# GpSimd splits the maxima and divides the sums; the batch chain is laid over more steps; maxima run 30 ahead

## The reference

```
x = x + gelu(layernorm(x) @ ctx^T) @ ctx
x = x + router over 8 experts (gelu MLP, weighted) of layernorm(x)
q = layernorm(x) @ Wq^T ; k, v = ctx @ Wk^T, ctx @ Wv^T          (16 heads of 16)
x = x + softmax(where(mask, q k^T + bias[bucket(distance)], -1e9)) v @ Wo^T
h = layernorm(x); e = argmax of a small router on h's last row of each batch
x = x + h + 0.3 * ((gelu(h @ W1[e] + b1[e]) @ W2[e] + b2[e]) @ Wo + bo)
```

## Time and profile before

| | |
|---|---|
| median of 3 runs | 736.22 us (727.66 to 737.24) |
| profiled execution | 738.62 us, span of the core 736.8 us |
| PE, DVE, ACT, POOL busy | 650.3, 357.2, 262.1, 96.6 us |
| attention loop (64 steps) | about 416 to 653 us |

### The profile page before, as it was taken

How to read it: one execution, slowest core, us unless ns; L and a number is a source line. 1 busy time by engine, 2 the same in 40 slices (tenths; PEclk the granted TensorE clock), 3 DMA queues, 4 the chain that set the end, 5 groups by cost and what they waited for, 6 DMA issues and landing times.

```text
span 736.8 us, 8966 instructions
## 1 busy us (share of the span) xinstructions
PE 650.3 (88%) x3020; PEld 383.9 (52%) x3021; DVE 357.2 (48%) x1115; ACT 262.1 (36%) x353; POOL 96.6 (13%) x102
## 2 busy tenths in 40 slices
PE   3999999999997768999697898989887988799996
PEld 2666666666665447899673333333342333243644
DVE  4324423003036872232274878868878788423302
ACT  1111111111122322344215666636643675562220
POOL 0000000000020003545401503001006000303000
PEclk9999999999998998999988999979986999899999
DMA  9993105103001135222239524153161000302031
GB/s 313 362 348 124 65 1 180 64 0 118 0 1 62 56 121 118 74 64 77 68 117 127 84 34 78 39 85 68 17 126 23 2 1 2 115 2 57 1 114 57
DMA packets 48131, 61.96 MB, mean 84 GB/s; under 512 B 7959, under 2 KB 41272, under 8 KB 47688
## 3 DMA queue, kind: packets, MB, share of 16 engines
q1 hardware_dynamic: 45944, 55.66, 28.7%
q0 software_dynamic: 2144, 5.77, 2.7%
HBM read 43.89 MB, written 10.93 MB: 74 GB/s over the span
## 4 chain that ended last, share of the span: by engine, by line
PE 72%; DVE 16%; issue 4%; DMA 3%; ACT 3%; POOL 1%; DVEq 0%; POOLq 0%; ACTq 0%; SPq 0%
PE ps L859 13%; PE ps L870 12%; PE ps L1416 8%; PE ps L1398 6%; PE ps L1301 5%; PE ps L1133 4%; PE ps L1021 4%; DVE arena L2098 4%; PE ps L1029 3%; PE ps L1124 3%; DVE arena L1801 2%; PE ps L943 2%; PE ps L1143 2%; PE ps L1324 1%; PE ps L1049 1%
## 5 line engine op out<-in xcount | busy, mean ns | idle before, releaser
L1626 ACT ACTIVATE arena<-ps 100x1024 f32<-100x1024 f32 x128 | 124.6, 1021 | 81.8 <-PE ps L1398 81.6
L2098 DVE TENSOR_REDUCE arena<-ps 128x1 f32<-128x400 f32 x256 | 131.4, 566 | 32.2 <-PE ps L1301 30.2
L859 PE MATMUL ps<-xnT,arena 128*128 128x512 f32 x208 | 102.0, 616 | 0.9 <-DVE xnT L1686 0.9
L870 PE MATMUL ps<-arena 128*128 128x256 f32 x416 | 99.7, 384 | 0.0
L870 PEld LDWEIGHTS ps<-arena 128*128 128x128 f32 x416 | 80.6, 194 | 33.6 <-issue 25.0
L1454 ACT ACTIVATE arena<-ps 128x512 f32<-128x512 f32 x52 | 31.1, 597 | 175.8 <-PE ps L859 175.8
L1301 PE MATMUL ps<-arena 97*128 97x400 bf16 x256 | 79.4, 354 | 11.3 <-DVE arena L2098 8.2
L1398 PE MATMUL ps<-arena 100*100 100x512 bf16 x256 | 81.3, 403 | 0.7 <-DMA arena<-arena 0.5
L1416 PE MATMUL ps<-arena 100*32 100x512 f32 x512 | 76.3, 659 | 0.5 <-ACT arena L1626 0.5
L1301 PEld LDWEIGHTS ps<-arena 97*128 97x128 bf16 x256 | 20.9, 99 | 89.5 <-DVE arena L2098 56.8
L1686 DVE COPY xnT<-ps 128x512 f32<-128x512 f32 x16 | 10.4, 687 | 100.3 <-PE ps L832 100.3
(11 more groups left out here) (228 smaller groups left out, 701.9 us busy)
## 6 DMA issues: line engine op xcount, KB each, us to landing
arena<-in_W SPq DMA_DIRECT2D x16, 512.0 KB, 8.8
arena<-in_ctxT SPq DMA_DIRECT2D x4, 1664.0 KB, 8.5
arena<-in_ctxN SPq DMA_DIRECT2D x4, 1664.0 KB, 12.8
arena<-arena SPq DMA_DIRECT2D x48, 128.0 KB
arena<-in_pW SPq DMA_DIRECT2D x8, 512.0 KB, 4.3
last_k_parts<-arena SPq DMA_DIRECT2D x24, 100.0 KB, 1.8
arena<-last_k_parts SPq DMA_DIRECT2D x8, 300.0 KB
x_tok<-in_x SPq DMA_DIRECT2D x4, 512.0 KB, 9.3
```

The costliest lines, as they stand in the source:

```text
L859: ins = pe.matmul(ps[:, 4 + k % 2, :], ctxT_s[:, b % 2, c, f * P:f * P + P], xnT[:, c, S * b:S * b + S], start=(c == 0), stop=(c == KC - 1))
L870: ins = pe.matmul(ps[:, b % 2 * 2 + t // 2, t % 2 * D:t % 2 * D + D], hid[:, (k - 2) % 4, t * P:t * P + P], ctxN_s[:, b % 2, f, :], start= ...
L1626: act.activation(pexp2[0:KT, c % 4, :, :], ps[0:KT, 2 + 2 * (c % 2):4 + 2 * (c % 2), :], ACT.Exp).then_inc(f_pe, 1)
L2098: dve.tensor_reduce(nm2[:, h, j:j + 1], ps[:, FAST.bank(x), 0:KF], AX.X, ALU.max, negate=True).then_inc(s_by["dve"], 1)
```

## The change

Three things, in the fast way alone. LEAD goes from 28 to 30. GpSimd gets an order of its own by steps: it splits the maxima of the units from 2 on (the units 0 and 1 stay with VectorE), multiplies by the reciprocals that VectorE still takes (divide; turn_back waits for it), and does the last queries' split, the normalised rows and the final sums (in two halves) at given steps. The chain goes over more steps: projections at 3 and 5, roots at 6, 7, 9, 11, normalised rows at 12, turns at 13 and 14, sums at 13 and 15. nm2, rl2 are doubled. The router's loads stand behind maxima row 4 instead of 10.

```diff
-LEAD = 28
+LEAD = 30
+OWN_SPLITS = 2
...
-CHAIN = {3: ("project", 0), 4: ("project", 1), 10: ("turn4", 0), 12: ("turn4", 1)}
-ROOTS_AT = 4
+CHAIN = {3: ("project", 0), 5: ("project", 1), 13: ("turn4", 0), 14: ("turn4", 1)}
+ROOTS_AT = (6, 7, 9, 11)
+NORM_AT, BASE_AT = 12, (13, 15)
...
@@ SyncE, fast_way @@
-                    if w == 10:
+                    if w == 4:
                         router_weights()
...
@@ VectorE, maxima(m) @@
+                    if n == 0 and m >= 2 * MU:
+                        dve.wait_ge(s_nm, m // MU - 1)
+                    dve.tensor_reduce(nm2[:, m // MU % 2, h, j:j + 1], ps[:, FAST.bank(x), 0:KF], AX.X, ALU.max, negate=True).then_inc(s_by["dve"], 1)
...
-                def normalise(i):
-
-                    lo = i % 2 * DK
+                def invert_sums(i):
+
                     dve.wait_ge(f_oc, i + 1)
-                    cf.step(dve, dve.reciprocal(rl2[:, :, :], vt2[:, i % 2, :, DK:DK + 1]))
-                    cf.step(dve, dve.tensor_tensor(vn2[:, i // 2 % 2, :, lo:lo + DK], vt2[:, i % 2, :, 0:DK],
-                                                   rl2.broadcast_to([P, S // VW, DK]), ALU.mult))
+                    cf.add(dve.reciprocal(rl2[:, i % 2, :, :], vt2[:, i % 2, :, DK:DK + 1]))
+                    inverted[i] = cf.n

                 def turn_back(i):
...
+                    dve.wait_ge(f_div, i + 1)
...
-                    if t == 0 and u + 1 < UNITS:
+                    if t == 0 and 1 <= u + 1 < OWN_SPLITS:
                         split_maxima(u + 1)
...
@@ GpSimd @@
+            def fast_way():
+                steps = Chain(s_split)
+
+                def split_maxima(w):
+
+                    pool.wait_ge(s_by["dve"], FAST.taken(("max", MU * w + MU - 1))[1])
+                    pool.wait_ge(s_made, FAST.made(("max rows", w - 1)))
+                    nv, rv = nm2[:, w % 2, :, :].rearrange("p h j -> p j h"), nr2.rearrange("p h j -> p j h")
+                    steps.step(pool, pool.tensor_copy(nmb2[:, :, 0, :], nv))
+                    steps.step(pool, pool.tensor_tensor(rv, nv, nmb2[:, :, 0, :], ALU.subtract))
+                    steps.step(pool, pool.tensor_copy(nmb2[:, :, 1, :], rv))
+                    pool.tensor_tensor(nmb2[:, :, 2, :], rv, nmb2[:, :, 1, :], ALU.subtract).then_inc(s_nm, 1)
+
+                def divide(i):
+
+                    lo = i % 2 * DK
+                    pool.wait_ge(f_dv, inverted[i])
+                    pool.tensor_tensor(vn2[:, i // 2 % 2, :, lo:lo + DK], vt2[:, i % 2, :, 0:DK],
+                                       rl2[:, i % 2, :, :].broadcast_to([P, S // VW, DK]), ALU.mult).then_inc(f_div, 1)
+
+                late = [x for st in range(STEPS) for x in extras(st) if x[0] == "products"]
+                for use in range(KC * (B - 1) - len(late)):
+                    split_query(use, steps)
+                for st in range(STEPS):
+                    u, t = divmod(st, CT)
+                    if t == 0 and OWN_SPLITS <= u + 1 < UNITS:
+                        split_maxima(u + 1)
+                    if t == 1 and u >= 1:
+                        divide(u - 1)
+                    for x in extras(st):
+                        if x[0] == "products":
+                            split_query(KC * (x[1] - 1) + x[2], steps)
+                    for b in range(B - 1):
+                        n = st - (b + 1) * NG * CT
+                        if n == NORM_AT:
+                            norm(b)
+                        if n in BASE_AT:
+                            k = BASE_AT.index(n)
+                            base(b, TB // 2 * k, TB // 2 * k + TB // 2, steps)
+                divide(UNITS - 1)
+                norm(B - 1)
+                base(B - 1, 0, TB, steps)
```

More of the change, by code:

```diff
@@ L386, in build @@
         pexp2 = view([4, 2, S]); vt2 = view([2, S // VW, VW]); vn2 = view([2, S // VW, VW]); mrow2 = view([2, S], BF16)
-        nm2 = view([HG, TB]); nr2 = view([HG, TB]); rl2 = view([S // VW, 1])
+        nm2 = view([2, HG, TB]); nr2 = view([HG, TB]); rl2 = view([2, S // VW, 1])
         nmb2 = view([TB, VW // HG, HG], BF16)
@@ L536, in build @@
         f_oc = sem("values_fast_taken")
+        f_div = sem("values_fast_divided")
         s_made = sem("pieces_made")
@@ L544, in build @@
         s_out = sem("rows_stored")
-        def per(i, k):
-            return i * k
+        inverted = {}
         block = ctx.enter_context(nc.Block())
@@ L2097, in maxima @@
                     dve.wait_ge(s_made, FAST.made(x))
-                    dve.tensor_reduce(nm2[:, h, j:j + 1], ps[:, FAST.bank(x), 0:KF], AX.X, ALU.max, negate=True).then_inc(s_by["dve"], 1)
+                    if n == 0 and m >= 2 * MU:
+                        dve.wait_ge(s_nm, m // MU - 1)
+                    dve.tensor_reduce(nm2[:, m // MU % 2, h, j:j + 1], ps[:, FAST.bank(x), 0:KF], AX.X, ALU.max, negate=True).then_inc(s_by["dve"], 1)
                 def split_maxima(w):
@@ L2104, in split_maxima @@
                         dve.wait_ge(s_made, FAST.made(("max rows", w - 1)))
-                    nv, rv = nm2.rearrange("p h j -> p j h"), nr2.rearrange("p h j -> p j h")
+                    nv, rv = nm2[:, w % 2, :, :].rearrange("p h j -> p j h"), nr2.rearrange("p h j -> p j h")
                     cf.step(dve, dve.tensor_copy(nmb2[:, :, 0, :], nv))
@@ L2176, in fast_way @@
                     if t == 1 and u >= 1:
-                        normalise(u - 1)
+                        invert_sums(u - 1)
                     if t == 2 and u >= 1 and u % 2 == 0:
@@ L2185, in fast_way @@
                     for b in range(B - 1):
-                        n = st - (b + 1) * NG * CT - ROOTS_AT
-                        if 0 <= n < 4:
-                            roots_share(b, n)
+                        n = st - (b + 1) * NG * CT
+                        if n in ROOTS_AT:
+                            roots_share(b, ROOTS_AT.index(n))
                     if st == LOGIT_STEP + 1:
@@ L2191, in fast_way @@
                     max_steps(maxima_of_step(st, 2, HG))
-                    if t == 0 and u + 1 < UNITS:
+                    if t == 0 and 1 <= u + 1 < OWN_SPLITS:
                         split_maxima(u + 1)
                 turn_values(UNITS - 1)
-                normalise(UNITS - 1)
+                invert_sums(UNITS - 1)
                 turn_back(UNITS - 1)
@@ L2249, in _, with split_query @@
                     store_answers(j)
-            steps = Chain(s_split)
-            for use in range(KC * (B - 1)):
+            pool.wait_ge(s_list, 1)
+            near = pool.value_load(lst_i[0:1, 33:34], min_val=0, max_val=NC - 1)
+            def split_query(use, steps):
                 b, m = 1 + use // KC, use % KC
@@ L2259, in _, with norm @@
                 pool.tensor_tensor(qp_of[b][:, 2, m, :], f, qp_of[b][:, 1, m, :], ALU.subtract).then_inc(s_qs, 1)
-            for b in range(B):
+            def norm(b):
                 pool.wait_ge(s_lnst, B + b + 1)
@@ L2264, in _, with base @@
                 ins.then_inc(s_ln, 1)
+            def base(b, lo, hi, steps):
                 pool.wait_ge(s_ln, 3 * B + b + 1)
-                if b == 0:
+                if b == 0 and lo == 0:
                     pool.wait_ge(s_w4, 16 * 6)
                     steps.step(pool, pool.tensor_scalar(bo_s[:, :], bo_s[:, :], 0.3, None, ALU.mult))
-                rows = slice(TB * b, TB * b + TB)
+                rows = slice(TB * b + lo, TB * b + hi)
                 steps.step(pool, pool.tensor_tensor(x_tok[:, rows, :], x_tok[:, rows, :], xn[:, rows, :], ALU.add))
-                pool.tensor_tensor(x_tok[:, rows, :], x_tok[:, rows, :], bo_s.unsqueeze(1).broadcast_to([P, TB, D]), ALU.add).then_inc(s_base, 1)
+                ins = pool.tensor_tensor(x_tok[:, rows, :], x_tok[:, rows, :], bo_s.unsqueeze(1).broadcast_to([P, hi - lo, D]), ALU.add)
+                if hi == TB:
+                    ins.then_inc(s_base, 1)
+                else:
+                    steps.step(pool, ins)
@@ new lines, in general_way @@
+            def general_way():
+                steps = Chain(s_split)
+                for use in range(KC * (B - 1)):
+                    split_query(use, steps)
+                for b in range(B):
+                    norm(b)
+                    base(b, 0, TB, steps)
+            def fast_way():
+                steps = Chain(s_split)
+                def split_maxima(w):
+                    pool.wait_ge(s_by["dve"], FAST.taken(("max", MU * w + MU - 1))[1])
+                    pool.wait_ge(s_made, FAST.made(("max rows", w - 1)))
+                    nv, rv = nm2[:, w % 2, :, :].rearrange("p h j -> p j h"), nr2.rearrange("p h j -> p j h")
+                    steps.step(pool, pool.tensor_copy(nmb2[:, :, 0, :], nv))
[9 more added lines that the diff above has]
+                for use in range(KC * (B - 1) - len(late)):
+                    split_query(use, steps)
+                for st in range(STEPS):
[8 more added lines that the diff above has]
```

(10 more changed lines are left out.)

## The result

The changed kernel takes 703.44 us (median of four runs, 703.10 to 703.64) against 736.66 for the kernel before (727.66 to 737.24 in this comparison). The ratio is 0.958, 95% interval 0.950 to 0.965: 4.2% faster. The profiled execution is the one of 703.10 us, with a span of 701.3.

The account below looks back on a forecast made before the run. PE, busy 88% of the span, was taken as the bound, losing time to idling and a lowered clock. 738.6 - 16.6 (idle: 24.8 gone, 8.2 new) - 13 (clock) = 709.0 us; range 700 to 727.

Parts of the forecast that it names:

- Part 1: Split on GpSimd and LEAD 30: split takes 1.04 us, ending before PE wants it; 17.5 us go, 2.8 stay.
- Part 2: Division on GpSimd: 0.59 us, covered because VectorE's turn_back stands in the next step; costs nothing.
- Part 3: Chain over more steps: 3.8 and 3.5 us of idle go; 1.2 for projections and 2.0 for roots come.
- The 3.8, 3.5 and the three 0.99: PE idle to go: 3.8 at three projections, 3.5 behind GpSimd's final sums; the 0.99 split waits are within the 17.5.
- part 5: Two more maxima ahead of the loop: -0.3 us, against at most +1.2 for ScalarE's copies; together put at 0.
- Part 4: Normalisation behind step 12's split on GpSimd: PE's turn in step 13 waits 1.1 us in two batches, 2.2 new.
- The clock: Attention loop at 0.92 of full clock, 19.0 us missing: one fall of 5 us left, 13 us won.
- 2.27 place: Batch border where projection, turning, residual, statistics and split share a step: PE waits 0.54 + 0.74 + 0.99 us, three times.
- Everything closes: Rival: the roots' wider spacing makes them cost nothing and no clock fall is left: 701 us, chance 0.10.
- The falls come back: Rival: clock lost at the normalisation behind the split or the roots, three or four falls: 722 us, chance 0.17.
- The split fills its slack: Rival: at 2.84 us a split, PE waits the old 0.98 in 14 groups again: 730 us, chance 0.08.
- the slow case: Rival: small GpSimd operations cost like 512-column ones, split 3.78 us, five clock falls: 759 us, chance 0.07.

Follow-up runs that it names:

- lead_28: The changed kernel with LEAD back at 28, all else as changed: 724.19 us.
- split_8_more: The changed kernel with the first cast of every split on GpSimd done nine times in place of once: 735.21 us.
- divide_on_vector: The changed kernel with the multiplication by the reciprocals back on VectorE: 705.33 us.
- norm_first: The changed kernel with the normalisation ahead of step 12's split on GpSimd, not behind it: 700.47 us.
- norm_late: The changed kernel with the normalisation one step later in GpSimd's queue, behind the division of step 13: 720.18 us.
- splits_on_vector: The changed kernel with all 16 splits on VectorE, at their old place behind the late pair of reductions: 710.86 us.
- early_on_vector: The changed kernel with all splits on VectorE, directly behind the early pair of reductions and ahead of the turning of the values: 706.31 us.
- chain_alone: The kernel before with only the chain's new steps and the router loads behind maxima row 4: 725.40 us.
- old_chain: The changed kernel with the chain at its old steps; splits and divisions stay on GpSimd, LEAD 30: 704.91 us.

## Why the prediction was right, and what it missed

**Part 1**, the split and LEAD. I took 0.2 us an operation and 0.08 between two, 1.04 in all; measured 0.20 to 0.23, 1.07 from the first start to the last end (454.89 to 455.96). "16 columns are 0.04 us", by the rate per column, did not hold: the rate fits from 256 columns up and says nothing of 16. The 0.2 itself was a choice between 0.10 and 0.61 with no row behind it, and that it came out so near is luck. The fit for the division missed little: 0.62 for 0.59. "Late next: the bank of the second late product, about 0.2 x 14 = 2.8": measured 0.22 in 12 waits, 2.6, and one of 0.25 for GpSimd's split. Theory A of lead_28 and split_8_more put a number on the slack, and both waits came.

**Part 2**, nothing for the division: at most 1.9 us (divide_on_vector), a little more than nothing.

**Part 3**, the chain. The 3.8, 3.5 and the three 0.99 went. Two terms were mis-sized. "I take 0.4 x 3 = 1.2 us new" for the second projection's bank: no such wait shows. "I take 1.0 for each" for the roots, 3.0 in all, 2.0 more than before: measured 0.35 in each of two batches and none in the third; spread over six steps they find room. Together 3.5 us too much; against it stands the routing's wait for ScalarE in the third batch, 1.14 where it had been 0.32, which part 5 had put at 0.

**Part 4**, the normalisation behind a split: 1.1 twice predicted, 1.15 twice measured, nothing in the third batch as said; norm_first took it away and got the 2.3 us back.

**The clock.** The forecast kept one fall, 5 us. None came in the loop of the profiled execution; the other three lie within 0.5 us of it at the same mean clock or a higher one (0.972 to 0.975), which speaks for none in them either. The step that failed is "near a 2.27 place, of which two in three had a fall": 0.22 and 1.15 us, the two waits of step 13, were followed by none. That this follows from their size is argued and not shown, for the other runs have no fixed size from which the clock falls (last section). The 19.0 us of clock, from 0.92, was also too large: by PE's busy time it was 15.8. So the clock gave 15.8 for the forecast's 13, idle time 19.3 for 16.6. Together that is 5.5 of the 5.9 us between 709.0 and the profiled 703.1; the other 0.4 is that the loop starts 0.4 us earlier.

**The rivals.** By its mechanism the run is nearer to "Everything closes", to which I gave 0.10, than to the forecast: the roots cost next to nothing and no fall is left. It lies 2.4 us above that rival's 701, since there were 2.8 us of clock left to win over the forecast and not 5. "The falls come back" takes waits like norm_late's. That norm_late's 720.18 is near this rival's 722 is chance: the rival had 13 us of clock and no new wait, norm_late has 9.9 of clock and 7.5 of waits. "The split fills its slack" and the slow case both asked for dear small operations; with a split of 3.2 us (split_8_more) the kernel is as slow as before. I had put the turn to a loss in idle time at 3.0 us a split; at 3.2 idle is still 2.0 below the kernel before (26.8 to 28.8), for the roots and banks cost 3.5 less than I had counted, and the normalisation's two waits came to 3.3 where my sum has 6.6. The rule of twice VectorE's time (the Trainium skill, "GPSIMD Engine Reference", § Performance versus the Vector engine, where it was measured at 2048 columns) doesn't hold at 16 columns here: four operations in 1.07 us against VectorE's 0.82, a factor of 1.3. At 256 columns it is 0.62 to 0.42 us, 1.5. The rule of the shared port (the Trainium skill, "SBUF — State Buffer", § Who interferes with whom) is agreed with once more: in step 9 one root operation on 4 columns ran 0.46 us beside the division. That is 0.3 us, not the 0.6 feared, and no wait of PE's followed.

```profile
495.52 0.46 DVE L2165 TENSOR_TENSOR root_squared<-rstd 128x4 f32<-128x4 f32 x1
```

## What to carry to other kernels

When an engine waits for a short serial tail at the end of another's queue, look at two things together: which of the tail's inputs comes last, and which engine runs the tail. Here the earlier input was worth 21 us by the medians with the tail on GpSimd (lead_28 against the changed kernel) and 5 with it on VectorE (splits_on_vector against early_on_vector). GpSimd was worth 3 to 8 with the early input (the two kernels with early splits on VectorE against theirs with GpSimd). With the late one it was 13 slower than VectorE (lead_28 against splits_on_vector, whose leads differ: splits_on_vector has 30 but starts its splits late, and no kernel with the new chain has 28 and the splits on VectorE). So moving the tail to the slower engine paid here only together with an earlier last input. Price the wait with the clock that goes after it: norm_late's 7.5 us of waiting cost 16.7 by the medians. And put a queue's short, urgent work and its long work in order of when each can start: the normalisation, ready 2.0 us before the split, stood behind it and cost 2.3.

## What the runs showed that I had not expected

The clock doesn't answer to equal waits equally. The split under the query work took 2.26 us of PE's time in the kernel before without a fall (at 449) and in chain_alone with one:

```profile
449.00 0.34 PE L1314 MATMUL ps<-eye_b,arena 128*32 128x128 bf16 x3 [2.26 <-DVE arena L2109]
```

```profile
448.56 0.50 PE L1314 MATMUL ps<-eye_b,arena 128*32 128x128 bf16 x3 [2.26 <-DVE arena L2109]
```

```profile
448.00:458.00 10.00, 9.44 (x34) 3.16 (x35) 6.00 (x14) 3.07 (x4) 0.26 (x1) 0.50 0.69 113
```

In splits_on_vector 2.06 us at the same place had none, while in split_8_more 1.75 us had one, and in old_chain three waits that come to 1.51 us had one behind one batch and none behind two. In the kernel before, the third 2.27 us place had none either. Nor does the clock wait for the end of a wait: in norm_late it was still whole up to 507.5 us and fell before 508, while the 3.50 us wait lasted to 509.02. What decides between equal waits is open.

The range of the kernel before, 727.66 to 737.24, has about the width of two falls of 5 us. Its executions in the three sets bear that out: those near 727 us had a mean granted clock of 0.962 to 0.967, those from 737 us up 0.942 to 0.951, and 0.015 of 737 us is 11 us. Which falls the shorter executions lacked isn't shown, since one execution was profiled. In split_8_more and lead_28 the falls behind the last groups held for 13 and 17 us, where the steps have no maxima products; in the kernel before the last one, among such steps too, held for 7.
